# Last attention of a two-layer decoder: routing, dispatch and experts of each batch two slots later

## What is computed

```python
x = _layernorm(x + _L1_xattn_ref(x, ctx, ctx, Wq, bq, Wk, bk, Wv, bv, Wo, bo))
x = _layernorm(x + _L1_ffn_ref(x, Wr, W1, b1, W2, b2))

# _L1_ffn_ref, K = 2, E = 8, capacity = int(256 / 8 * 1.25) = 40
probs = softmax(x @ Wr)
topk_probs, topk_experts = top_k(probs, K)
pos = how many earlier (token, choice) pairs of the batch went to the same expert
keep = pos < capacity
buf[expert, batch, pos] = x where keep
h = relu(buf @ W1 + b1)
y = h @ W2 + b2
out = sum over the two choices of y[expert, batch, pos] * keep * prob
```

## Time and profile before

| what | us |
|---|---|
| median of 3 runs | 790.64 |
| lowest, highest | 787.52, 794.8 |
| the profiled execution | 796.1 |
| its span, first to last instruction | 794.3 |
| PE busy in it | 719.1 |
| DVE busy in it | 489.1 |
| ACT busy in it | 412.9 |
| POOL busy in it | 290.0 |

### The profile page before, as it was taken

One profiled execution on the slowest core, in us unless ns is written; L12 is line 12 of the kernel. 1 busy time (PEld: TensorE's weight loads), 2 busy tenths in 40 slices (PEclk: granted clock), 3 DMA queues, 4 the chain that ended last, 5 costly groups with the idle time before them and its releaser, 6 DMA issues.

```text
span 794.3 us, 16402 instructions
## 1 busy us (share of the span) xinstructions
PE 719.1 (91%) x5852; PEld 542.2 (68%) x5852; DVE 489.1 (62%) x1297; ACT 412.9 (52%) x1047; POOL 290.0 (37%) x395
## 2 busy tenths in 40 slices
PE   8788889898897998999999989989888899999886
PEld 6565567575665765899898967758566455767665
DVE  4669777887977885444543455545455658583643
ACT  2234556657566677554544467555562545454311
POOL 0015355565555666110000036423350646363300
PEclk8869989999999999999999999999998756999999
DMA  8537451533727471000000000001011501000000
GB/s 235 126 69 179 123 128 43 122 83 88 161 46 205 112 214 57 2 1 1 1 1 1 1 1 4 1 2 41 4 38 54 185 26 31 2 2 9 8 7 7
DMA packets 25175, 48.11 MB, mean 61 GB/s; under 512 B 7264, under 2 KB 14192, under 8 KB 25096
## 3 DMA queue, kind: packets, MB, share of 16 engines
q1 hardware_dynamic: 24376, 45.66, 22.7%
q10 hardware_dynamic: 720, 1.41, 0.5%
HBM read 17.49 MB, written 0.52 MB: 23 GB/s over the span
## 4 chain that ended last, share of the span: by engine, by line
PE 60%; DVE 14%; issue 10%; ACT 8%; SPq 3%; POOL 2%; DMA 2%; POOLq 0%; ACTq 0%; DVEq 0%
PE SC L839 7%; PE G L550 7%; PE SC L826 7%; PE SC L769 5%; PE G L625 4%; PE SC L861 3%; PE G L938 3%; DVE shift_cols L1542 3%; PE SO L812 3%; ACT causal_probs L1154 2%; PE SO L893 2%; PE SC L743 2%; PE G L647 2%; SPq L1769 1%; PE G L577 1%
## 5 line engine op out<-in xcount | busy, mean ns | idle before, releaser
L1169 ACT ACTIVATE exps<-SC 128x512 f32<-128x512 f32 x192 | 114.4, 597 | 106.8 <-PE SC L769 106.1
L1542 DVE TENSOR_REDUCE shift_cols<-SC 128x2 f32<-128x512 f32 x192 | 129.5, 684 | 32.0 <-PE SC L743 31.5
L1621 POOL TENSOR_TENSOR rstd<-variance,consts 128x2 f32<-128x2 f32 (+1 forms) x48 | 36.8, 766 | 266.0 <-DVE variance L1234 263.0
L1689 POOL TENSOR_TENSOR VB<-exps 128x256 f32<-128x256 f32 x128 | 95.7, 756 | 59.4 <-ACT exps L1169 58.6
L1143 ACT ACTIVATE hidden<-SC,cols 128x256 f32<-128x256 f32 x128 | 53.6, 471 | 65.4 <-PE SC L826 65.3
L1711 POOL TENSOR_TENSOR causal_probs<-causal_probs,inverse 128x256 f32<-128x256 f32 x64 | 51.6, 828 | 68.9 <-DVE inverse L1555 68.9
L1576 DVE SCALAR_TENSOR_TENSOR R<-SC,small,R 128x128 f32<-128x128 f32 x128 | 39.0, 346 | 54.0 <-PE SC L839 53.3
L1154 ACT ACTIVATE causal_probs<-SC,negmax 128x128 f32<-128x128 f32 (+1 forms) x128 | 52.3, 424 | 37.1 <-DVE negmax L1550 37.0
L769 PE MATMUL SC<-stacked_q,stacked_k 100*128 100x256 f32 x256 | 66.9, 344 | 3.5 <-DMA stacked_q<-shift_rows 1.9
L839 PEld LDWEIGHTS SC<-ffn_w,hidden 128*128 128x128 f32 x512 | 66.0, 192 | 5.3 <-issue 1.8
L839 PE MATMUL SC<-ffn_w,hidden 128*128 128x128 f32 x512 | 67.6, 276 | 0.0
(11 more groups left out here) (257 smaller groups left out, 1504.5 us busy)
## 6 DMA issues: line engine op xcount, KB each, us to landing
stacked_k<-k_hi SPq DMA_DIRECT2D x64, 128.0 KB, 2.4
stacked_q<-q_hi SPq DMA_DIRECT2D x64, 128.0 KB, 2.4
ffn_w<-in_ffn_w SPq DMA_DIRECT2D x16, 512.0 KB, 4.8
stacked_k<-k_lo SPq DMA_DIRECT2D x32, 128.0 KB, 2.4
stacked_q<-q_lo SPq DMA_DIRECT2D x32, 128.0 KB, 2.5
packed_k<-U SPq DMA_DIRECT2D x48, 32.0 KB, 1.9
packed_q<-YN SPq DMA_DIRECT2D x48, 32.0 KB, 1.9
a_weights<-in_a_li SPq DMA_DIRECT2D x3, 256.0 KB, 7.4
```

What stands on the lines that cost most here:

```text
L1169: fn(exps[:, n % EXPS, :, :].rearrange("p t q -> p (t q)"), SC[1][:, n % 2, :, :].rearrange("p t q -> p (t q)"), ACT.Exp, scale=ATTENTIONS ...
L1542: v.tensor_reduce(shift_cols[:, n // UNIT % 4, :, n % UNIT], SC[0][:, n % 2, :, :], axis=AX.X, op=ALU.max, negate=True).then_inc(head_max, 1)
L1689: v.tensor_tensor(kept[n % EXPS].rearrange("p t q -> p (t q)"), exps[:, n % EXPS, 0, :], exps[:, n % EXPS, 1, :], ALU.add).then_inc(kept_r ...
```

## The change

In `mix`, every step from the turning of the norm on is two larger, on all five engines; steps 1 to 3 (projection, residual, norm, and POOL's bias and first deviation) stay. The last slot of the loop moves by two as well. Nothing else is changed.

```diff
--- before.py
+++ after.py
@@ -120,7 +120,7 @@
-LAST = LX_AT + HEADS * (NB - 1) + OUT_AFTER + 31
+LAST = LX_AT + HEADS * (NB - 1) + OUT_AFTER + 33
 
@@ -899,9 +899,9 @@
-                    yield 5
+                    yield 7
                     normal_transposed(b, 8, X[b])
-                    yield 6
+                    yield 8
                     wait_weights(pe, "m1")
@@ -909,14 +909,14 @@
-                    yield 12
+                    yield 14
                     pe.wait_ge(chosen_ready[b], 2)
-                    yield 15
+                    yield 17
                     pe.wait_ge(dispatch_ready[b], 1)
@@ -925,7 +925,7 @@
-                            yield 16 + 2 * m
+                            yield 18 + 2 * m
                             if m == 0:
@@ -938,7 +938,7 @@
-                        yield 17 + 2 * m
+                        yield 19 + 2 * m
                         if m < 2:
@@ -959,7 +959,7 @@
-                        yield 27 + t
+                        yield 29 + t
                         for m in range(2):
@@ -1114,19 +1114,19 @@
-                    yield 5
+                    yield 7
                     tokens_turned(b, 8)
-                    yield 7
+                    yield 9
                     act.wait_ge(logits_shifted[b], 2)
-                    yield 15
+                    yield 17
                     copied(("buf", b), BUF[:, :], lambda g: g[:, :])
-                        yield 16 + 2 * m
+                        yield 18 + 2 * m
                         wait_emptied(act, ("up1", b, m))
-                            yield 17 + 2 * m
+                            yield 19 + 2 * m
                             copied(("PWT", b, m), PWT[:, 2 * m:2 * m + 2, :].rearrange("p a b -> p (a b)"),
@@ -1484,20 +1484,20 @@
-                    yield 6
+                    yield 8
                     g = wait_filled(dve, ("r1", b))
-                    yield 8
+                    yield 10
                     dve.wait_ge(logits_exp[b], 2)
-                    yield 9
+                    yield 11
                     chosen(b, expd1[b], E1, onehot1[b], chosen1[b], 2).then_inc(chosen_ready[b], 1)
-                    yield 12
+                    yield 14
                     g = wait_filled(dve, ("pos", b))
@@ -1510,7 +1510,7 @@
-                    yield 13
+                    yield 15
                     dve.wait_ge(dispatch_ready[b], 1)
@@ -1519,22 +1519,22 @@
-                            yield 16 + 2 * m
+                            yield 18 + 2 * m
                             g = wait_filled(dve, ("up1", b, m))
-                            yield 17 + 2 * m
+                            yield 19 + 2 * m
                             g = wait_filled(dve, ("y", b, m - 1))
-                        yield 27 + t
+                        yield 29 + t
                         last = residual_part(("comb", b, t), b, t, X[b])
-                    yield 30
+                    yield 32
                     normalise(b, R[b], Z[b]).then_inc(final_ready[b], 1)
@@ -1670,7 +1670,7 @@
-                    yield 28
+                    yield 30
                     inverse_deviation(b)
@@ -1822,7 +1822,7 @@
-                    yield 31
+                    yield 33
                     sp.wait_ge(final_ready[b], 1)
```

## The result

The changed kernel took 801.36 us (median of 4 runs) against 792.4 for the kernel before beside it: ratio 1.0096, interval 1.0054 to 1.0138. Measured again in 12 runs the ratio was 1.0052 (1.0016 to 1.0088), about 4 us. The kernel before against itself gave 0.9995 (0.9969 to 1.0022). The two intervals overlap from 1.0054 to 1.0088, which is a loss of 4 to 7 us; I had forecast 1.0. The time lay above my range. By the second set the loss is about four times what I worked out, by the first between seven and eight times. Of the 9.8 us between my 791.6 and the measured 801.4, 1.8 are the kernel before itself, whose median went from 790.64 to 792.4 with its fourth run.

A forecast was written before the change was run, and what follows sets the result against it. PE, busy for 91% of the span, was taken as the bound. Terms +1.5 - 0.5 - 0.5 - 0.7 + 1.0 + 0.2 = +1.0 us on the median 790.64 gave 791.6 us; range 786.4 to 797.5.

The forecast's parts named there:

- (a): Before the first gathering: two more slots of heads alone at half clock, +1.3, gathering itself +0.2; together +1.5 us.
- (e): Batch 2's projection, right behind its gathering, waits for DVE's late divide: +1.0 us; batch 1: 0.
- (b): Batch 0's router matmuls (L909) no longer wait for the bank of cross_values: -0.5 us.
- (c): Output projection behind the gathering covers ACT's copy to slot_tokens at batches 0 and 1: -0.5 us.
- (d): Head scores near 710 us no longer wait for DVE, busy with the slot masks: -0.7 us.
- (f): Tail, last head product to batch 2's second-layer matmuls: 18.0 us instead of 16.7, 1.1 of it moved work; +0.2 us.
- the first: Rival: clock rises ahead of the first gathering, sum -1.7 us, 788.9 us; chance 0.2.
- The second: Rival: clock stays at half for 6.8 us past the gathering, +3.4, sum +4.4 us, 795.0 us; chance 0.15.
- The rule of the Trainium skill beside this rival: PE's clock is throttled by default and activity releases it; thinner work in front would give 795.0 us.
- The third: Rival: divide late at all three places, sum +4.1 us, 794.7 us; chance 0.12.

The follow-up runs named there:

- late_choice_12: Changed kernel with the choice of experts on DVE at step 12 instead of 11; ratio 1.007 against the kernel before.
- late_dispatch: Kernel before with everything from the positions on two slots later, but turning, router, softmax and choice at their old steps; ratio 1.0073.
- short_fill_late: Changed kernel plus two 512-column matmuls ahead of PE's wait for batch 3's masks, one ahead of its slot_tokens wait; ratio 1.0016 against before.
- late_3_slots: The changed kernel's steps moved three slots later instead of two; ratio 1.0045 against the kernel before.
- fill_narrow: Kernel before with two extra 64-column matmuls, results thrown away, in each slot r18 to r45; median 813.0 us beside 794.5.
- late_again: The changed kernel itself measured once more, with a second trace; ratio 1.0052 against the kernel before.

## Why the prediction was wrong

By its own steps:

(a) Two slots of heads alone ahead of the first gathering: this is the step that failed, together with the second interval under (e). I had +3.06 for the slots, -0.5 from (b), so +2.6 on the first interval; it was +3.9 and +3.3 in the two traces. That the clock is at half around the gathering was right (PEclk 0.50 behind the start of L923, its row 3.78 us). But the 3.06 us, a price at half clock without waits, are not what came: the time at half clock in the interval hardly grew (15.8 and 15.1 us against 15.1 and 15.2), PE's busy time grew by only 1.3 and 1.2 us, and the time that PE stood still, put at nothing, by 2.6 and 2.0. The waits are those at 667 and 670; late_choice_12 shows that the second of them comes from the choice of experts on DVE, and that the first, in the chain of inverse, check and key sums, does not. That the sum was near the mark is thus luck in part. Since late_dispatch has fewer waits, more time at half clock and the same 29.4 us, the cause of the size stays open between the two. I had +0.2 for the gathering itself and near half clock; it took 0.6 to 0.7 more than before, and I had not followed how long the clock stays at half behind it.

The sum leaned on a reading of PE's waits that was too short: behind slot_tokens and the values tile I wrote "little more than that", but the longest group of all stood there too, and 1.0 us for the maxima:

```profile
PE G L923 <- DVE slot_of L1510: 2.8, 2, 2.0
```

(b) right: the wait of L909 for the values tile is gone. (c) right: three of four waits for slot_tokens are gone, 1.9 to 0.7 us.

(d) wrong: the wait for shift_cols near 710 did not go, it is 0.35 us instead of 0.72, and a new one of 1.44 stands at 670.15. I had followed only the masks on DVE, not the choice of experts, which moves with them.

(e) wrong the other way: the projection of batch 2 followed the gathering without a wait (716.34 to 718.19). I had the divide end 6.9 us behind the start of the positions (712.18); it ended 5.7 behind it (717.91), since the masks were over after 2.7 us instead of 3.2 and the refine took 0.41 instead of 0.93. The wait came at batch 3, 0.62 us. But PE had by then lost more in front of it: from the combination to the positions 3.4 us instead of 2.4. The second interval is 1.3 us longer where (a), (c) and (d) together gave 0.8 shorter. About 0.9 us went at that place by the choice of experts (late_dispatch and late_choice_12), and about 0.8 by the longer stretch at half clock behind the first gathering; the wait of 0.72 near 710 gave some back.

(f) right: 18.2 us from the last head product to the second layer of batch 2, forecast 18.0; third and fourth interval together 1.1 us shorter, by my sum 0.8.

The second interval and (a) miss by 2.1 and 1.0 us, the third and fourth interval by -0.3: my 1.0 and the missing 2.8 make 3.8 us, the mean of what the two traces show where the clock behind the last gathering is equal (3.4 and 4.1), and about what the second set of runs says. What the first set of four runs has above that is scatter, or the clock stretch that short_fill_late points to; the runs don't tell these apart.

Of the rivals, the first did not come: the clock was at half from 668.3 to 682.0. The second had the right sign and nearly the size (795.0), but its mechanism came only in part: the clock rose 3.9 and 4.2 us behind the start of the first gathering, some 0.3 us behind its end, not 6.8 us behind it, and in before 2.4 and 2.6 us behind the start. The rule of the Trainium skill beside this rival pointed the right way. The third, a divide that is late at all places, shows in late_3_slots (3.7 us for OB) and hardly in the changed kernel (0.6). My range ended 2.5 us above the second rival; it held no case in which two losses come together, nor one with the clock behind the last gathering.

## What to carry to other kernels

When a chain of steps is moved in a schedule of slots, follow every engine's share of the chain, the small operations too, to what stands there already: here a choice of experts, ten short DVE instructions, came behind a refine, and head scores waited for the maxima behind it, 1.44 us at one place and some 0.9 at another. What is saved at the far end has to be read from that end: slots that were not bound by the engine don't pay back at its rate. And a difference of under 1% in a kernel whose clock falls and rises needs the distances between landmarks of several traces; single spans differed by 7 us between two executions of the same kernel. Even that needs the time at half clock beside it: the distance from the first projection to the end was 145.6 us in both traces of before, but the first interval alone varied by 2.9 us between kernels whose order up to there was the same.

## What the runs showed of the hardware

With heads alone PE's clock stood at half for 3.4 to 27 us at a time, although PE was busy for about nine tenths of such a stretch or more (6.90 of 6.90 us in the earlier trace rows); for 13.6 us behind 654.7 in the changed kernel it was full with the same kind of work. In fill_narrow PE was busy for 27.30 of 27.30 us at 0.50. The same order of PE's instructions behind the last gathering took 24.3 us with the clock full (late_again) or 29.4 with 13.6 us at half (late_choice_12). The wait of 2.0 us just ahead was filled in three kernels and none of the three traces has a slow stretch behind it; that the wait is the cause is supported by this and not shown. Two head products that ran side by side in 0.43 us ran one behind the other once a wait of 0.35 us had come between them (709.91 and 710.76 in the changed kernel).
